# Ranking tokens for a mixture of experts: counts kept during attention, ranks added up by TensorE, one weight split moved

## The reference, cut to what matters

```python
x = x + tanh(g_xattn) * attention(layernorm(x), ctx, ctx)      # softmax(q k^T / 4) v, then Wo
xf = layernorm(x).reshape(2048, 256)
logits = xf @ Wg                                               # 16 experts
_, topi = top_k(logits, 2)
gates = softmax(where(mask(topi), logits, -inf))
for e in range(16):
    h = silu(xf @ W1[e] + b1[e]) * (xf @ W11[e] + b11[e])      # 256 -> 512
    y = y + (h @ W2[e] + b2[e]) * gates[:, e, None]
z = silu(xf @ Ws1 + bs1) * (xf @ Ws11 + bs11) @ Ws2 + bs2      # shared, 256 -> 1024 -> 256
x = x + tanh(g_ffn) * (y + z)
```

## Time and profile before

| what | value |
|---|---|
| median of three runs | 610.73 us (610.62 to 611.23) |
| the profiled execution's own time | 612.34 us |
| its span, first to last instruction | 610.0 us |
| PE busy | 558.2 us (91%) |
| DVE busy | 348.0 us (57%) |
| POOL busy | 338.8 us (56%) |
| ACT busy | 213.5 us (35%) |
| mean granted TensorE clock | 0.983 |

### The profile page before, as it was taken

How to read it: one execution, slowest core, us unless ns; L and a number is a source line. 1 busy time by engine, 2 the same in 40 slices (tenths; PEclk the granted TensorE clock), 3 DMA queues, 4 the chain that set the end, 5 groups by cost and what they waited for, 6 DMA issues and landing times.

```text
span 610.0 us, 11682 instructions
## 1 busy us (share of the span) xinstructions
PE 558.2 (91%) x3146; PEld 443.7 (73%) x3147; DVE 348.0 (57%) x845; ACT 213.5 (35%) x740; POOL 338.8 (56%) x284
## 2 busy tenths in 40 slices
PE   5789889899987999958999999999999999989897
PEld 4356656656655778846888888888888888868786
DVE  5467777777664582213656555655565555322763
ACT  0677776776786111111222222222122222121110
POOL 4477788888879316563444755474444730056620
PEclk9799999999999999988999999999999999989999
DMA  7562000000120602223556787558555210122323
GB/s 250 236 249 85 27 27 18 26 26 17 27 79 18 240 13 93 87 87 124 181 195 201 251 285 254 195 189 296 198 188 209 86 43 27 36 78 77 91 62 115
DMA packets 32319, 76.05 MB, mean 125 GB/s; under 512 B 4896, under 2 KB 21408, under 8 KB 29344
## 3 DMA queue, kind: packets, MB, share of 16 engines
q1 hardware_dynamic: 12944, 51.52, 23.5%
q10 hardware_dynamic: 16272, 15.74, 8.2%
q0 software_dynamic: 3072, 8.39, 4.3%
HBM read 54.93 MB, written 18.61 MB: 121 GB/s over the span
## 4 chain that ended last, share of the span: by engine, by line
PE 70%; DVE 10%; POOL 8%; issue 7%; ACT 2%; DMA 2%; DVEq 0%; ACTq 0%; POOLq 0%
PE mid L646 13%; PE big L627 7%; PE big L629 7%; PE big L628 7%; PE work L402 5%; POOL sorted_x L1332 5%; PE mid L637 3%; PE big L431 3%; PE big L551 3%; PE big L549 3%; PE big L550 3%; PE last L567 3%; PE work L567 2%; PE work L417 2%; PE work L611 2%
## 5 line engine op out<-in xcount | busy, mean ns | idle before, releaser
L774 ACT ACTIVATE last<-arena 128x512 f32<-128x512 f32 x47 | 28.3, 602 | 183.9 <-DVE arena L1142 183.9
L709 ACT ACTIVATE arena<-big,nmax 128x128 f32<-128x128 f32 x256 | 90.3, 398 | 3.7 <-DVE nmax L880 3.7
L646 PE MATMUL mid<-dring,arena 128*128 x376 | 88.9, 379 | 0.0
L627 PE MATMUL big<-u_hi,xsT_hi 128*128 x188 | 82.3, 438 | 0.9 <-issue 0.9
L1142 DVE TENSOR_TENSOR arena<-big,bring 128x512 f32<-128x512 f32 x47 | 32.5, 692 | 87.1 <-PE big L629 87.1
L1251 POOL TENSOR_TENSOR arena<-arena,rinv 128x1024 f32<-128x1024 f32 x32 | 60.7, 1898 | 25.8 <-DVE rinv L888 25.2
L1267 POOL TENSOR_TENSOR u_lo<-arena,u_hi 128x2048 fp32r<-128x2048 f32 x16 | 73.3, 4580 | 1.3
L629 PE MATMUL big<-u_hi,xsT_lo 128*128 x188 | 73.7, 392 | 0.0
L628 PE MATMUL big<-u_lo,xsT_hi 128*128 x188 | 73.3, 390 | 0.0
L646 PEld LDWEIGHTS mid<-dring,arena 128*128 128x128 f32 x376 | 67.8, 190 | 7.4
L709 ACT ACTIVATION_READ_ACCUMULATOR arena<-big,nmax 128x1 f32 x256 | 61.1, 239 | 0.0
(11 more groups left out here) (133 smaller groups left out, 1120.7 us busy)
## 6 DMA issues: line engine op xcount, KB each, us to landing
arena<-up_w_dram SPq DMA_DIRECT2D x16, 1024.0 KB, 7.6
bring<-expert_bias_dram SPq DMA_DIRECT2D x16, 640.0 KB, 5.3
dring<-down_w_dram SPq DMA_DIRECT2D x18, 512.0 KB, 3.4
sorted_y<-arena ACTq DMA_DIRECT2D x47, 128.0 KB, 1.8
arena<-sorted_x ACTq DMA_DIRECT2D x43, 128.0 KB, 2.1
sorted_x<-dring SPq DMA_DIRECT2D x3, 1536.0 KB, 8.4
dring<-up_w_dram SPq DMA_DIRECT2D x2, 1024.0 KB, 4.8
xf_all<-xfs SPq DMA_DIRECT2D x16, 128.0 KB, 2.0
```

Source lines behind the costliest of these rows:

```text
L627: mm(big[:, p, w, :], x_hi, u_hi[:, slot, o:o + HID], start=(k == 0), stop=False)
L646: i = mm(mid[:, 1, 0:D], gT[:, p, c, :], dring[:, slot, c * D:(c + 1) * D], start=(c == 0), stop=(c == HC - 1))
L709: i = nc.scalar.activation(probs[:, u % 2, h, :], big[:, u % 2, h // 4, (h % 4) * CTX:(h % 4 + 1) * CTX], ACT.Exp, bias=nmax[:, u % 2, h:h ...
```

## The change

Three things change.

1. `count(j)` adds a pair's one-hots (`oh`) and keeps a running sum over tiles (`cum`), three DVE instructions each. It runs in the pairs 2 to 7 for the pair two before, ahead of `choose_copy`; twice more behind attention.
2. PE multiplies the last running sum by ones first (`totals_ps`), and adds triangle times `oh` and ones times `cum` in one bank, so that the rank over all tiles leaves PE ready. DVE's sum over tiles goes; counts in blocks come from a division, a rounding by 2^23 and a maximum, and the sum over experts has a zero pad instead of copies. Positions come ahead of the table of blocks. PE's `shared_up` for chunks 2 and 3 is cut in halves around the router and the products.
3. POOL splits the second weight in one piece behind `keep_xfT(LAST)` and ahead of the scatters, instead of in quarters in pair 7.

```diff
+            def count(j):
+                link(v.tensor_tensor(oh[:, bass.ds(2 * j, 2), :], chosen[:, 0, bass.ds(2 * j, 2), :],
+                                     chosen[:, 1, bass.ds(2 * j, 2), :], ALU.add))
+                link(v.tensor_tensor(cum[:, bass.ds(2 * j + 1, 1), :], cum[:, bass.ds(2 * j, 1), :], oh[:, bass.ds(2 * j, 1), :], ALU.add))
+                ins = v.tensor_tensor(cum[:, bass.ds(2 * j + 2, 1), :], cum[:, bass.ds(2 * j + 1, 1), :],
+                                      oh[:, bass.ds(2 * j + 1, 1), :], ALU.add)
+                if isinstance(j, int) and j == LAST:
+                    ins.then_inc(onehots_ready, 1)
+                else:
+                    link(ins)
...
                     if behind and u == 3:
+                        if not (isinstance(j, int) and j < 2):
+                            count(j - 2)
                         choose_copy(j - 1)
                         choose(j - 1)
...
-            shared_up(0, 2)
+            shared_up(0, 2, [0])
             router(LAST)
-            shared_up(0, 3)
+            shared_up(0, 2, [1])
+            shared_up(0, 3, [0])
 
             pe.wait_ge(onehots_ready, 1)
-            mm(mid[:, 0, 0:TILES * E], const[:, C_TRI:C_TRI + P], rt[:, 0, :], start=True, stop=True)
-            mm(mid[:, 1, 0:TILES * E], const[:, C_ONE:C_ONE + P], rt[:, 0, :], start=True, stop=True).then_inc(rank_ps, 1)
+            mm(mid[:, 1, 0:E], const[:, C_ONE:C_ONE + P], cum[:, TILES, :], start=True, stop=True).then_inc(totals_ps, 1)
+            mm(mid[:, 0, 0:TILES * E], const[:, C_TRI:C_TRI + P], oh[:, :, :].rearrange("p t e -> p (t e)"), start=True, stop=False)
+            mm(mid[:, 0, 0:TILES * E], const[:, C_ONE:C_ONE + P], cum[:, 0:TILES, :].rearrange("p t e -> p (t e)"),
+               start=False, stop=True).then_inc(rank_ps, 1)
+            shared_up(0, 3, [1])
...
-            for b in range(2):
-                add_attention(LAST, b)
-                ln2_apply(LAST, b)
-                shared_hidden(0, [b])
+            add_attention(LAST, 0)
+            count(LAST - 1)
+            ln2_apply(LAST, 0)
+            shared_hidden(0, [0])
+            add_attention(LAST, 1)
+            ln2_apply(LAST, 1)
+            shared_hidden(0, [1])
             copy_xfT(LAST)
-            shared_hidden(0, [2])
             choose_copy(LAST)
             choose(LAST)
+            count(LAST)
+            v.tensor_tensor(gtmp[:, 0, :], top2[:, 1, :], top2[:, 0, :], ALU.subtract).then_inc(gate_exp_in, 1)
+            shared_hidden(0, [2])
...
+            dve.wait_ge(totals_ps, 1)
+            link(v.tensor_scalar(cnt[:, 0, :], mid[:, 1, 0:E], P / 2 - 0.5, 1.0 / P, ALU.add, ALU.mult))
+            link(v.tensor_scalar(cnt[:, 1, :], cnt[:, 0, :], ROUND, None, ALU.add))
+            link(v.tensor_scalar(pre[:, 0, PAD:], cnt[:, 1, :], -ROUND, 1.0, ALU.add, ALU.max))
+            cur, step = 0, 1
+            while step < E:
+                link(v.tensor_tensor(pre[:, 1 - cur, PAD:], pre[:, cur, PAD:], pre[:, cur, PAD - step:PAD + E - step], ALU.add))
+                cur, step = 1 - cur, 2 * step
+            ends, starts = pre[:, cur, PAD:], pre[:, cur, PAD - 1:PAD + E - 1]
+            dve.wait_ge(rank_ps, 1)
+            ins = v.scalar_tensor_tensor(out=r3(0), in0=starts.unsqueeze(1).to_broadcast([P, TILES, E]), scalar=float(P),
+                                         in1=mid[:, 0, 0:TILES * E].rearrange("p (t e) -> p t e", t=TILES), op0=ALU.mult, op1=ALU.add)
+            ins.then_inc(rank_taken, 1)
             shared_hidden(0, [3])
...
+            link(v.tensor_tensor(prod, chosen[:, :, :, :], r3(0).unsqueeze(1).to_broadcast([P, TOPK, TILES, E]), ALU.mult))
+            link(v.tensor_reduce(pos_f[:, :, :].rearrange("p k t -> p (k t)"), prod.rearrange("p k t e -> p (k t) e"), AX.X, ALU.add))
+            v.tensor_copy(pos[:, :, :], pos_f[:, :, :]).then_inc(pos_ready, 1)
...
-                    if split_first == 1:
-                        pool.wait_ge(raw_odd, 16)
-                        split(PIECES + u, raw_first, 1, u, UNITS)
...
-            pair(LAST, False, True, False, 1)
+            pair(LAST, False, True, False)
...
             keep_xfT(LAST)
 
+            pool.wait_ge(raw_odd, 16)
+            split(PIECES, raw_first, 1, 0, 1)
             pool.wait_ge(pos_ready, 1)
```

More of the change, by code:

```diff
@@ L128, in flamingo_layer @@
         top2 = sb("top2", [P, TOPK, TILES])
-        cnt = sb("cnt", [P, 6, E])
+        cnt = sb("cnt", [P, 2, E])
+        oh = sb("oh", [P, TILES, E])
+        cum = sb("cum", [P, TILES + 1, E])
+        pre = sb("pre", [P, 2, E // 2 + E])
         pos_f = sb("pos_f", [P, TOPK, TILES])
@@ L266, in flamingo_layer @@
         rank_ps = sem("rank_ps")
+        totals_ps = sem("totals_ps")
         rank_taken = sem("rank_taken")
@@ L535, in _, with shared_up @@
             pair(LAST, 1, False, False, True)
-            def shared_up(s, c):
+            def shared_up(s, c, halves=range(2)):
                 h, g = divmod(s, TILES // GROUP)
                 n = HC * s + c
-                if n >= 2:
+                if n >= 2 and 0 in halves:
                     pe.wait_ge(gsh_ready, n - 1)
@@ L544, in shared_up @@
                 x_lo = [xfT_lo[:, k, GROUP * P * g:GROUP * P * (g + 1)] for k in range(DC)]
-                for w in range(2):
+                for w in halves:
                     for k in range(DC):
@@ L551, in shared_up @@
                         i = mm(big[:, c % 2, w, :], w_lo, x_hi[k], start=False, stop=(k == DC - 1))
-                i.then_inc(sh_ps, 1)
+                if 1 in halves:
+                    i.then_inc(sh_ps, 1)
             def shared_ups(s):
@@ L978, in pair @@
                     if behind and u == 3:
+                        if not (isinstance(j, int) and j < 2):
+                            count(j - 2)
                         choose_copy(j - 1)
                         choose(j - 1)
+            v.memset(cum[:, 0, :], 0.0)
+            v.memset(pre[:, :, :], 0.0)
             v.memset(mhalf[:, :], -0.5).then_inc(half_ready, 1)
@@ L1010, in _ @@
             before = links[0]
-            LINKS = 2 * (2 * 2 + 2 * 2 + 4)
+            LINKS = 2 * (2 * 2 + 2 * 2 + 4 + 3)
             with dve.Fori(1, LAST // 2) as i:
@@ L1058, in _ @@
             choose(LAST)
+            count(LAST)
+            v.tensor_tensor(gtmp[:, 0, :], top2[:, 1, :], top2[:, 0, :], ALU.subtract).then_inc(gate_exp_in, 1)
+            shared_hidden(0, [2])
             def r3(i):
                 return rt[:, i, :].rearrange("p (t e) -> p t e", t=TILES)
-            ins = v.tensor_tensor(r3(0), chosen[:, 0, :, :], chosen[:, 1, :, :], ALU.add)
-            ins.then_inc(onehots_ready, 1)
-            v.tensor_tensor(gtmp[:, 0, :], top2[:, 1, :], top2[:, 0, :], ALU.subtract).then_inc(gate_exp_in, 1)
@@ L1068, in _ @@
-            shared_hidden(0, [3])
[L1069 to L1077, removed]
-            shared_hidden(1, [0])
@@ L1079, in _ @@
[L1079 to L1094, removed]
+            ROUND = float(1 << 23)
+            PAD = E // 2
+            dve.wait_ge(totals_ps, 1)
+            link(v.tensor_scalar(cnt[:, 0, :], mid[:, 1, 0:E], P / 2 - 0.5, 1.0 / P, ALU.add, ALU.mult))
@@ new lines, in _ @@
+            ins = v.scalar_tensor_tensor(out=r3(0), in0=starts.unsqueeze(1).to_broadcast([P, TILES, E]), scalar=float(P),
+                                         in1=mid[:, 0, 0:TILES * E].rearrange("p (t e) -> p t e", t=TILES), op0=ALU.mult, op1=ALU.add)
+            ins.then_inc(rank_taken, 1)
+            shared_hidden(0, [3])
+            dve.wait_ge(rank_taken, 1)
+            prod = rt[:, 1:1 + TOPK, :].rearrange("p k (t e) -> p k t e", t=TILES)
+            link(v.tensor_tensor(prod, chosen[:, :, :, :], r3(0).unsqueeze(1).to_broadcast([P, TOPK, TILES, E]), ALU.mult))
@@ L1103, in _ @@
             shared_hidden(1, [1])
[L1104 to L1114, removed]
             shared_hidden(1, [2, 3])
@@ L1338, in _ @@
             pool.wait_ge(sh_ps, HC * TILES // GROUP)
-            split(PIECES + UNITS, raw[:, 0, :], 0, 0, 1)
+            split(PIECES + 1, raw[:, 0, :], 0, 0, 1)
             pool.wait_ge(table_ready, 1)
@@ L1347, in split_expert @@
                 g.tensor_tensor(pool_mark[:, :], mhalf[:, :], mhalf[:, :], ALU.mult)
-                split(PIECES + UNITS + i - 2, raw[:, slot, :], slot, 0, 1)
+                split(PIECES + i - 1, raw[:, slot, :], slot, 0, 1)
             with pool.Fori(0, (E - 2) // 2) as i:
```

## The result

The changed kernel takes 621.38 us (median of four runs, 619.61 to 621.93) against 610.88 (610.62 to 611.23) of the kernel before in the same measurement: ratio 1.0182, 95% interval 1.0156 to 1.0208. It is 1.8% slower, 10.5 us. The forecast was 615.3 us, in the right direction, but with a range that ended at 619. The profiled execution of the changed kernel took 621.83 us, with a span of 620.0 against 610.0.

What follows compares the result with a forecast made beforehand. PE holds 70% of the chain of waits, with an 8.67 us gap at the scatters to win. Terms +9.6 +0.1 +0.1 -3.2 -2.0 = +4.6 on the 610.7 median gave 615.3 us, range 607 to 619.

Steps and rivals of the forecast that it cites:

- The delay of the pairs: Looped pairs 2 to 5 lose 2.4 us each, 9.6 in all; memsets at the start and last two pairs add 0.1 each.
- The hold in the loop: In each looped pair, POOL's running instructions hold DVE's three `count` additions, so L946 ends 2.4 us later.
- What the chain does next (row maximum, `add_attention`, key projection) moves by the same 2.4: In looped pairs 2 to 5, the steps behind L946 up to PE's key projection come 2.4 us later, 9.6 in all.
- The last two pairs: Pair 6 loses 2.35 us; in pair 7 the removed split quarters pay for one count; entered as +0.1 us.
- The hold behind attention: POOL's whole split holds the first addition of `count(7)` 4.5 us; one-hots complete at 214.85, PE idles 5.8 us.
- Where scatters and PE meet: Scatters start 3.2 us earlier and keep their 48.3 us, so rows are back at 272.9, together with PE.
- The low clock from 276 to 280: PE's half-speed clock behind the gap at the scatters goes, as no idle time remains there: -2.0 us.
- (a): Rival: nothing is held and the additions hide in DVE's 1.25 us wait; -13.9 us, 597 us; chance 0.08.
- (b): Rival: additions are held in the pairs, but the long split doesn't hold DVE behind attention; -2.7, 608 us; chance 0.13.
- (c): Rival: held, but the third addition slips ahead of POOL's L1260; pairs cost 4.4, sum -0.6, 610.1 us; chance 0.11.
- (d): Rival: pairs 6 and 7 don't pay for each other (+2.3), weight loads slow the scatters (+1); 618.6 us; chance 0.10.
- The cost of weight loads under the scatters: Down weights of experts 1 and 2 load during the scatters; nothing entered, at worst 1 us for slower scatters.

Runs made afterwards that it cites:

- Experiment 1: The changed kernel with the three additions of `count` written as sums over an axis of two, one input each: 604.41 us, ratio 0.9887 to the kernel before.
- experiment 7: The changed kernel with one-input counts and the subtraction of the two best logits moved behind the table of blocks: 599.25 us, ratio 0.9809 to the kernel before.
- experiment 6: The changed kernel with PE's transpositions of unit 0's probabilities done twice in pairs 2 to 6 alone: 616.90 us, ratio 1.0104 to the kernel before.
- Experiment 3: The changed kernel with the second weight's split in quarters in pair 7 again: 618.59 us, ratio 1.0100 to the kernel before.

## Why the prediction was right or wrong

The direction, the hold and most steps were right. The delay of the pairs was forecast at 9.8 us and came to 13.9, as the slower key projection was left out of it; the earlier rows were mis-sized by 1.4 us.

- **The hold in the loop: right.** Additions at 1.4, 0.8 and 1.2 us were forecast; 1.47, 0.83 and 1.27 came. L955 ended 2.26 us later, for which I had 2.4. Experiment 1 shows that it is the form with two inputs in SBUF that is held, and not the number of linked instructions. That one input alone would be enough is not shown: L953, a copy, took 0.77 us, and L1096 of experiment 7, a `tensor_scalar`, 3.13. The prediction was also loose with the rows of before: the longest held instruction there is the L857 of before with 1.36 us; 1.9 us is only the length of POOL's longest. And that L857 is a `tensor_scalar` with one tensor as input, so it is not a case of two inputs. A hold of that length came only with the change: L962 took 1.92 us at 190.29, under a `normalise` of 1.90.
- **"What the chain does next (row maximum, `add_attention`, key projection) moves by the same 2.4": the step that failed.** It moved by that, and then the key projection itself took 1.1 to 1.3 us more in three places, and the matmuls behind it some tenths, since PE had waited longer and came back at 1.2 GHz. At pair 7's output projection the changed kernel is 13.85 us later (209.32 against 195.47), where 9.8 was forecast. The missing 4.1 is the low clock: it cost 4.8 us in this execution by the pairs' lengths in experiment 6, less 0.5 by which this execution reached pair 1's copy of the logits earlier (64.13 against 64.65). With the doubling, experiment 6 takes 616.9 us, 5.1 less than the changed kernel beside it and within 1.6 of the forecast. I had the earlier trace rows with a low clock behind an idle time of 2.81 us, used it behind attention, and didn't ask what each 2.4 us of delay makes of PE's wait of 0.9 to 1.4 us in the loop.
- **The last two pairs: right in sum.** Pair 7 gave back 1.79 us by the copies of the logits (15.61 us after those of pair 6 against 17.40), where the forecast had 1.85. The agreement is in part luck, since the clock was low in pair 7 (0.63 from 204 to 208 us), which the forecast doesn't have; no run isolates what that cost.
- **The hold behind attention: right.** With 13.9 us taken off, the one-hots were complete at 214.4 (214.85 forecast), PE idle 5.46 (5.8), positions at 222.6 (222.0), and the scatters start at 222.9 (222.4). Experiment 3 shows the cause.
- **Where scatters and PE meet: off by 1.4 us.** The rows were to be read at 272.9; it was 274.3. PE came to the end of its shared work half a us late, and then waited 0.85 us for DVE's addition to x, a wait that the gap of 8.67 us had covered before and that I had left out.
- **The low clock from 276 to 280: right**, 2.1 us back (12.1 us late at the rows, 10.0 at the end).
- Sum: forecast 9.8 - 3.2 - 2.0 = 4.6; measured 13.9 - 1.8 - 2.1 = 10.0.
- Rivals: (a) nothing held and (b) only the short ones held are refuted by the trace, (c) too, as the third addition was held in each looped pair (1.19 to 1.27 us); (d), slower still, was nearest in time, for another reason than the ones it named. The cost of weight loads under the scatters didn't show: they took 46.7 us from first scatter to POOL's next instruction, 1.6 less than before.

Left open: why an idle time of PE of about 1.9 us is followed by a low clock in one pair and not in another. No run was made for it.

## What to carry to other kernels

Before a few small VectorE instructions go into idle time on a critical engine, look what GpSimd does there. In these traces the ones with two inputs in SBUF (and copies and `tensor_scalar` from SBUF to SBUF of 4 and 16 columns, though not of one) could last until the end of GpSimd's present instruction, 4.51 us at the most; writing the same sum as a reduction over one input took that away. A long GpSimd instruction belongs where no such instruction is on the path. And a delay on another engine that lengthens a wait of TensorE can cost twice: once as delay, and once more by the clock behind it.

## What the runs showed of the hardware that was not expected

- A `tensor_reduce` that adds pairs (128 x 16 from 128 x 32) takes 0.19 us beside any of POOL's instructions, as long as the free addition, and is never held in eight executions each.
- The hold lasts as long as POOL's instruction, up to the longest seen, 4.49 us, for an output of 32 columns.
- The low clock in the pairs came behind idle times of 1.87 to 2.35 us, and not each time: 3.24 us for the eight matmuls behind 1.87 in one execution, where in the pair just ahead it was 1.99 behind 1.95.
- More matmuls made the kernel 5.1 us faster (experiment 6).
